# How many experts ahead the token gathers run: four or three

## What is computed

```python
x = x + xattn0(layernorm(x), ctx)     # 16 heads of 8
x = x + ffn0(layernorm(x))            # shared expert + 7 routed, top 2 of 7, hidden 352
x = x + xattn1(layernorm(x), ctx)     # two attentions, an LSTM over 64 steps, a feed-forward
x = x + ffn1(layernorm(x))            # top-1 mixture of 8 experts, hidden 512
```

```python
capacity = int(1.25 * 2048 / 8)       # 320 token slots for each of the 8 experts
combine, dispatch = top1_gate(tokens, wg, capacity)
dispatched = einsum('sec,sm->ecm', dispatch, tokens)
h = relu(einsum('ecm,emf->ecf', dispatched, w1) + b1[:, None, :])
expert_out = einsum('ecf,efm->ecm', h, w2) + b2[:, None, :]
combined = einsum('sec,ecm->sm', combine, expert_out)
```

## Time and profile before

| | us |
|---|---|
| median of 3 runs | 713.92 |
| lowest and highest | 712.63, 714.38 |
| the profiled execution | 712.63 |
| its span in the trace | 710.8 |

### The profile page before, as it was taken

How to read it: one execution, slowest core, us unless ns; L and a number is a source line. 1 busy time by engine, 2 the same in 40 slices (tenths; PEclk the granted TensorE clock), 3 DMA queues, 4 the chain that set the end, 5 groups by cost and what they waited for, 6 DMA issues and landing times.

```text
span 710.8 us, 16741 instructions
## 1 busy us (share of the span) xinstructions
PE 666.9 (94%) x6582; PEld 568.9 (80%) x6582; DVE 449.8 (63%) x1177; ACT 336.8 (47%) x914; POOL 121.0 (17%) x221
## 2 busy tenths in 40 slices
PE   6699989999999999998999999899999999998995
PEld 2478779898898888886777777699999999964784
DVE  5489848747946755769999999543334344453453
ACT  1589862324222222238888887545555454410320
POOL 2225850022000000004311000000000000003774
PEclk8899999999999999999999999899999999988999
DMA  7600200000000000013422200000000001031210
GB/s 247 199 20 17 67 3 1 1 1 1 1 1 0 1 1 1 1 57 91 106 68 70 68 8 5 1 2 1 1 16 14 19 1 27 11 86 39 76 48 29
DMA packets 30088, 25.03 MB, mean 35 GB/s; under 512 B 3887, under 2 KB 26801, under 8 KB 29762
## 3 DMA queue, kind: packets, MB, share of 16 engines
q1 hardware_dynamic: 28418, 20.91, 10.6%
q0 software_dynamic: 1600, 3.15, 1.5%
HBM read 19.33 MB, written 5.51 MB: 35 GB/s over the span
## 4 chain that ended last, share of the span: by engine, by line
PE 80%; DVE 9%; issue 4%; SPq 3%; ACT 1%; DMA 1%; POOL 1%; POOLq 0%; DVEq 0%
PE SC L703 16%; PE PT L713 12%; PE MI L630 5%; PE SC L890 5%; PE PT L620 5%; PE SC L611 3%; PE SC L808 3%; PE SC L980 3%; PE SC L850 2%; PE SC L855 2%; PE PJ L593 2%; PE SC L814 2%; PE SC L811 2%; PE PT L861 2%; DVE kexp L1278 2%
## 5 line engine op out<-in xcount | busy, mean ns | idle before, releaser
L1112 ACT ACTIVATE big<-SC 128x512 f32<-128x512 f32 x88 | 52.5, 598 | 144.6 <-PE SC L703 144.5
L713 PEld LDWEIGHTS PT<-wd,big 128*128 128x128 f32 (+1 forms) x768 | 90.2, 191 | 2.8 <-issue 0.4
L713 PE MATMUL PT<-wd,big 128*128 128x128 f32 (+1 forms) x768 | 90.7, 274 | 0.0
L1439 DVE TENSOR_TENSOR big<-SC,big 128x512 f32<-128x512 f32 (+1 forms) x88 | 60.5, 689 | 41.7 <-PE SC L703 32.4
L703 PE MATMUL SC<-xP,wgP 128*128 128x512 f32 x264 | 78.8, 406 | 0.7 <-DVE big L1439 0.3
L703 PE MATMUL SC<-xP,wuP 128*128 128x512 f32 x264 | 74.6, 391 | 0.0
L630 PEld LDWEIGHTS MI<-vblk,PTs 128*64 128x64 f32 x1536 | 49.8, 139 | 11.2 <-ACT oT L1059 2.8
L703 PEld LDWEIGHTS SC<-xP,wuP 128*128 128x128 f32 x264 | 49.6, 188 | 10.9
L630 PE MATMUL MI<-vblk,PTs 128*64 128x18 f32 x1536 | 54.2, 213 | 3.9 <-ACT big L1064 1.7
L1054 ACT ACTIVATE PTs<-PT 128x512 f32<-128x512 f32 x96 | 52.2, 595 | 7.6 <-PE PT L620 6.5
L620 PE MATMUL PT<-ident,sc 128*128 128x128 f32 x384 | 54.0, 285 | 0.6 <-ACT sc L1049 0.6
(11 more groups left out here) (255 smaller groups left out, 1322.7 us busy)
## 6 DMA issues: line engine op xcount, KB each, us to landing
kvs<-in_ctxT SPq DMA_DIRECT2D x32, 64.0 KB, 2.0
w1s<-in_e1w SPq DMA_DIRECT2D x8, 256.0 KB, 2.9
w2s<-in_e1w SPq DMA_DIRECT2D x8, 256.0 KB, 3.2
wg<-in_wg SPq DMA_DIRECT2D x1, 1408.0 KB, 9.1
wu<-in_wu SPq DMA_DIRECT2D x1, 1408.0 KB, 12.0
wd<-in_wd SPq DMA_DIRECT2D x2, 512.0 KB, 14.1
x_mid<-X SPq DMA_DIRECT2D x1, 1024.0 KB, 5.1
X<-x_mid SPq DMA_DIRECT2D x4, 256.0 KB, 4.3
```

What stands on the lines that cost most here:

```text
L713: last = pe.matmul(PT[:, e % 2, t * P:t * P + P], h[0:w, t * P:t * P + P], wd[0:w, e, c, :], start=(c == 0), stop=(c == 2))
L1112: act.activation(sg[a % 2], SC[:, a % 2, :], ACT.Silu).then_inc(s["silu_done"], 1)
L1439: last = dve.tensor_tensor(hT[e % 2][0:w, c, :], SC[0:w, 2 + a % 2, :], sg[a % 2][0:w, :], ALU.mult)
```

## The change

The constant `AHEAD` goes from 4 to 3.

```diff
 BURST = 17
-AHEAD = 4
+AHEAD = 3
 WARM_LSTM = 1
```

## The result

| | before | after |
|---|---|---|
| median of 10 runs, us | 713.62 | 716.70 |
| lowest and highest | 711.58, 714.52 | 715.41, 720.71 |
| the profiled execution | 712.63 | 715.08 |
| its span | 710.8 | 713.3 |

The ratio after to before is 1.0055 with a 95% interval of 1.0038 to 1.0074: slower by 2.7 to 5.3 us. The medians differ by 3.1 us, the spans of the two profiled executions by 2.5.

What follows compares the result with a forecast made beforehand. PE work almost without a break, then scatters released by VectorE, was taken to bound the kernel. PE's 3.09 us lag at expert 7 gave +3.1 us on the median 713.92: 717.0 us, range 714.9 to 718.9.

Steps and rivals of the forecast that it cites:

- (1) wait for the stored rows: Expert 3's two gathers stand behind POOL's wait for the stored output rows, which landed long before; cost 0.
- (2) POOL idle before the first scatter: Expert 4's three gathers go after expert 0's two scatters; POOL idles from 664.3 to 668.7, losing three slots.
- PE's lag: PE's whole delay against its old schedule at each expert's token transposes, not to be added; 3.09 us at expert 7.
- PE's single waits at 5, 6, 7: PE's separate waits for gathers at the transposes of experts 5, 6 and 7: 1.0, 1.6 and 0.3 us.
- last scatter: End of POOL's queue: the tail keeps its five scatters and shifts with PE's lag, to a start at 709.4; +3.1 us.
- step 3: POOL's queue from expert 4's gathers on: scatters of e, then gathers of e+4, each round shifted by the lost slots.
- The bounds: Near and far ends from shorter or longer POOL slots and landings: last gather starts 693.47 or 695.01, +2.4 or +4.7 us.
- steps of 1.37 us: POOL's time from a gather's start to the next issue, among scatters; 1.37 us taken from five steps in the trace.
- the +2.4 and +3.1: Range of the sum if gathers were slow only beside VectorE additions with two SBUF inputs, as the skill's rule says.
- A: Rival, not slower: POOL's mean slot is 1.14 us or less, gathers catch up, PE never waits; 713.9 us, chance 0.10.
- C: Rival, somewhat slower: a deciding gather lands late, 3.9 us for the last one, lag 4.8, 718.7 us; chance 0.08.
- B: Rival, much slower: PE's clock falls to 1.2 GHz at expert 7's wait, up to 9.4 us more, 726.4; chance 0.02.

Runs made afterwards that it cites:

- wait_first: Kernel before, with only the wait for the stored output rows moved ahead of expert 3's gathers; median 713.37 us, ratio 1.0006.
- gap_kept: Changed kernel, but after ten gathers and POOL's idle wait the other ten gathers go out in one run, then all 20 scatters; 714.72 us, ratio 1.0008.
- ahead8: Kernel before with AHEAD raised from 4 to 8, so all 20 gathers go ahead of all scatters; median 713.88 us, ratio 0.9989.
- tail: Kernel before, with expert 6's releases taken block by block, two blocks in PSUM banks of their own; median 713.29 us, ratio 0.9995.
- tail2: Kernel before, with expert 6's releases and expert 5's first taken block by block and VectorE reordered around expert 6; median 711.93 us, ratio 0.9970.
- ahead2: Kernel before with AHEAD lowered from 4 to 2; median 741.27 us, ratio 1.0402.
- ahead2_warm: Lead of two, with 7 or 20 filling matmuls on PE ahead of each token transpose from expert 3 on; 739.27 us, ratio 1.0343 to the kernel before.

## Why the prediction was right

It forecast 717.0 us, from 714.9 to 718.9; the median is 716.7. That the medians differ by just the forecast 3.1 us is partly luck: the profiled executions give 2.8, and the middle of the ratio gives 3.9. By its steps, as intervals against the kernel before (PE's against its first transposes, which stand 0.33 us earlier after, 656.74 against 657.07):

| step | forecast | measured |
|---|---|---|
| (1) wait for the stored rows | 0 | 0 (wait_first) |
| (2) POOL idle before the first scatter | about 4.1 | 4.47 |
| PE's lag at expert 4 | 0.16 | 0.07 |
| at expert 5 | 1.16 | 1.01 |
| at expert 6 | 2.78 | 2.42 |
| at expert 7 | 3.09 | 2.79 |
| PE's single waits at 5, 6, 7 | 1.0, 1.6, 0.3 | 0.81, 1.25, 0.23 |
| last scatter | +3.1 | +2.8 |

- The mechanism is the forecast one. PE waits for the gathers of experts 5, 6 and 7, POOL waits for nothing between expert 0 and expert 5, and the tail has its old shape behind a lagging PE.
- The terms were a little too large. From the first scatter to the last gather the queue took 25.21 us (668.38 to 693.59), 0.2 less than laid out: the mean step after a gather among scatters was 1.34 us (13.38 in ten steps) and not 1.37. And PE began 0.04 us after the landing and not 0.14 as at the first transposes. Together this is the 0.3 at the last gather. The third gather of expert 6 landed in 2.83, taken as 2.9, which touches that expert's lag alone.
- Step 2 holds: idle time ahead of a gather delays it, and it makes 3.7 of the 7.8 us by which the last gather starts later. It is one of two parts; the other, three more scatters ahead, is in the layout of step 3. What gap_kept rejects is that the idle slots alone would give the time.
- The 4.1 us of idle time was a slip: the forecast's own times, 664.3 to 668.7, give 4.4. The bounds' last starts, 693.47 and 695.01, come out as 693.43 and 695.05 by their own steps, which moves neither +2.4 nor +4.7.
- The steps of 1.37 us were read too simply. Two of the kernel before's seven gathers among scatters took 1.01 us (672.67 and 679.51), not 1.04 to 1.14. In the ten profiled executions a gather that directly follows a scatter takes 1.04 to 1.05 us with no two-operand addition (L1635) beside it, and one that follows a gather 0.99 to 1.01 (123 of them). The fifteen that follow a gather and took 1.02 us or more, up to 1.15, all overlap such an addition; 23 others overlap one and took no longer. The gather of the changed kernel at 686.94 (1.07 us) has this row of VectorE beside it:

```profile
686.54 0.60 DVE L1635 SCALAR_TENSOR_TENSOR big<-b2r,gate,big 128x128 f32<-128x128 f32 x2
```

- The Trainium skill ("GPSIMD Engine Reference", section "8. Key points") states contention between GpSimd and VectorE instructions that have two SBUF inputs. The prediction's word that the trace does not bear this out went too far. The longest gathers fit it, the gathers directly behind a scatter have a longer time without it, and the measured +2.8 lies between the +2.4 and +3.1 that the prediction gave for it. No kernel here took the additions away, so contention is not shown as the cause.
- Of the rivals, A needed a mean slot of 1.14 us up to expert 6's third gather; it was 1.33 (668.38 to 686.94 in 14 slots). C did not occur: the gathers that PE waited for landed in 2.2 to 2.83 us. B did not occur in the changed kernel, whose longest wait in the stretch was 1.25 us. But the argument against it was weaker than it looked. It rested on a clock of 1.00 in 706.00 to 707.20 of one execution; in the same window the clock was 0.72 in ahead8 (row below) and 0.68 in tail, although PE's last matmul ended there about a microsecond later than in the kernel before.
- The whole time gives no finer answer. The ratio's middle is 3.9 us, more than the 2.8 of the profiled execution. Two of the ten runs took 719.8 and 720.7 with mean clocks of 0.964 and 0.963, against 0.970 to 0.977 in the others. The kernel before has such runs too (717.8 us at 0.965 and 718.3 at 0.963 among those run beside the experiments), so they do not come from the change alone. No trace covers them, and what slowed them stays open.

## What to carry to other kernels

When one queue carries both prefetches and results, write it out row by row: a prefetch behind a result waits for that result's producer. What counts is when each prefetch starts, and both the rows ahead of it and the waits among them go into that; compare it with the time at which its data is wanted. A lead that just hides the landings is enough (between four and eight no difference can be told here); one step less costs little (+2.8 us), and the next closes a loop from landing to landing (+29.0 us). Where the tail is a row of issues of 1.29 us behind one release, releasing its first rows sooner gained 1.5 us (tail2), and the longer lead gained nothing (ahead8).

## What the runs showed of the hardware that was not expected

The clock can be lower right behind the first wait for gathers, a stretch in which these kernels have PE do the same work. In ahead8 (windows, then PE's timeline):

```profile
660.00:664.00 4.00, 3.47 (x11) 1.70 (x10) 0.55 (x1) 1.33 (x3) 2.99 (x3) 0.73 0.30 87
...
706.00:707.20 1.20, 0.00 (x0) 0.00 (x0) 0.00 (x0) 0.00 (x0) 0.98 (x1) 0.72 0.08 28
```

```profile
656.56 0.61 PE L969 MATMUL PT<-ident,wu 128*128 128x128 f32 x3 [2.09 <-DMA wu<-rows_in,home]
657.70 3.65 PE L980 MATMUL SC<-xsT,w1s 128*128 128x320 f32 x8 [0.53 <-ACT xsT L1204]
```

The same eight matmuls took 2.42 us in the changed kernel, behind a wait of 1.86 us:

```profile
657.88 2.42 PE L980 MATMUL SC<-xsT,w1s 128*128 128x320 f32 x8 [0.53 <-ACT xsT L1204]
```

tail shows the same (3.85 us, clock 0.74 in 660 to 664, wait of 2.23). It costs these two executions over a microsecond and explains why their intervals from first to last are longer than their scatters' spacing says. They had the longest first waits of the ten profiled executions (2.09 and 2.23 us against 0.86 to 2.05). But whether it is the wait's length or its moment that decides can't be told from these: in ahead2 a wait of 2.84 us was followed by a block of 1.91 us and one of 3.32 us was not, and in ahead2_warm a wait of 1.81 us was followed by a block of 1.83 us.

Work given to PE to fill a wait is no sure remedy. In ahead2_warm it went with a new fall of the clock (0.66 in 676 to 680) where ahead2, with 3.32 us of plain waiting, had 1.00. What decides between them stays open.

Where no two-operand addition of VectorE stands beside it, a gather directly behind a scatter takes 1.04 to 1.05 us and the next slot begins about 1.35 us after its start; directly behind a gather it takes 0.99 to 1.01 and the slot is 1.30 to 1.31. A scatter takes 1.02 us directly behind a gather and 0.98 to 1.00 behind a scatter. Why the change from one to the other costs this was not tried.
